# Moving two of the four value tiles behind the next step's keys, unpacking nibbles in four operations, and adding the last rows one block sooner

## The reference

```python
x = x + _layernorm(_L0_attn_ref(_layernorm(x), W_Q, W_K, W_V, W_O, b_Q, b_K, b_V, b_O))
x = x + _layernorm(_L0_ffn_ref(_layernorm(x), gate_W_packed, gate_scales, up_W_packed, up_scales,
                               down_W_packed, down_scales))
# attention: 16 heads of 128, causal softmax
q, k, v = x @ W_Q + b_Q, x @ W_K + b_K, x @ W_V + b_V
z = softmax(where(causal, q @ k.T / sqrt(128), -100000.0)) @ v
out = z @ W_O + b_O
# MLP, 2048 hidden: the weights are 4-bit codes, two to an int word, with a scale per 32
low, high = W_packed & 15, W_packed >> 4 & 15       # low nibble first
W = NVFP4_LUT[interleaved(low, high)] * scales
out = (gelu_tanh(x @ Wg.T) * (x @ Wu.T)) @ Wd.T
```

## Time and profile before

| | |
|---|---|
| median of 3 timed runs | 1555.29 us (1555.06 to 1555.84) |
| the profiled execution: its own time | 1557.55 us |
| the profiled execution: span of the trace | 1555.8 us |
| PE busy | 1539.1 us, 99% of the span |
| DVE busy | 1080.1 us, 69% |
| ACT busy | 985.8 us, 63% |
| POOL busy | 714.2 us, 46% |
| DMA, mean rate | 122 GB/s |
| granted TensorE clock | 0.999 of full speed |

### The profile page before, as it was taken

One profiled execution on the slowest core, in us unless ns is written; L12 is line 12 of the kernel. 1 busy time (PEld: TensorE's weight loads), 2 busy tenths in 40 slices (PEclk: granted clock), 3 DMA queues, 4 the chain that ended last, 5 costly groups with the idle time before them and its releaser, 6 DMA issues.

```text
span 1555.8 us, 25706 instructions
## 1 busy us (share of the span) xinstructions
PE 1539.1 (99%) x8136; PEld 1326.5 (85%) x8136; DVE 1080.1 (69%) x3116; ACT 985.8 (63%) x2449; POOL 714.2 (46%) x1069
## 2 busy tenths in 40 slices
PE   8999999999999999999999999999999999999998
PEld 7888888888888888888888888888788888888887
DVE  5666777777777777677777777757667676675765
ACT  7887777767776777677777776654444444444443
POOL 6673455444455455445445445433333333333333
PEclk9999999999999999999999999999999999999999
DMA  5653444444444444444444444681211121112101
GB/s 161 185 163 101 141 153 136 137 152 146 146 150 139 143 145 154 140 138 147 144 141 142 146 142 148 213 309 63 94 51 60 54 68 39 57 55 68 54 28 41
DMA packets 173415, 190.48 MB, mean 122 GB/s; under 512 B 17888, under 2 KB 143840, under 8 KB 173280
## 3 DMA queue, kind: packets, MB, share of 16 engines
q1 hardware_dynamic: 173280, 188.84, 37.9%
HBM read 105.93 MB, written 82.84 MB: 121 GB/s over the span
## 4 chain that ended last, share of the span: by engine, by line
PE 87%; DMA 4%; ACT 3%; DVE 3%; SPq 2%; issue 1%; POOL 0%; DVEq 0%; ACTq 0%
PE fbank L790 15%; PE fbank L788 15%; PE fbank L789 15%; PE obank L788 7%; PE obank L790 7%; PE obank L789 7%; PE ubank L788 5%; PE ubank L790 5%; PE ubank L789 5%; PE ubank L813 3%; PE fbank L899 3%; DMA turned_scratch<-turned 2%; DMA back<-turned_scratch 1%; SPq L542 1%; ACT probs L674 1%
## 5 line engine op out<-in xcount | busy, mean ns | idle before, releaser
L1378 POOL TENSOR_TENSOR pT_lo<-back,pT_hi 128x512 fp32r<-128x512 f32 x128 | 165.9, 1296 | 284.0 <-ACT pT_hi L742 284.0
L788 PE MATMUL fbank<-xnT_hi,wqk_hi 128*128 128x512 f32 x640 | 249.8, 390 | 0.2 <-DVE xnT_lo L972 0.2
L790 PE MATMUL fbank<-xnT_hi,wqk_lo 128*128 128x512 f32 x640 | 249.4, 390 | 0.0
L789 PE MATMUL fbank<-xnT_lo,wqk_hi 128*128 128x512 f32 x640 | 249.4, 390 | 0.0
L1338 POOL TENSOR_SCALAR probs<-probs,rsum 128x128 f32<-128x128 f32 (+1 forms) x512 | 210.5, 430 | 11.4 <-DVE rsum L995 6.5
L685 ACT ACTIVATE w_raw<-fbank 128x512 f32<-128x512 f32 x128 | 76.6, 598 | 211.9 <-PE fbank L790 211.9
L987 DVE CUSTOM_DVE_ANT_0 probs<-ubank,mask 128x128 f32<-128x128 f32 (+1 forms) x512 | 156.3, 356 | 30.5 <-PE ubank L790 28.2
L1358 POOL TENSOR_TENSOR v_lo<-probs,v_hi 128x512 fp32r<-128x512 f32 x64 | 83.1, 1299 | 175.5 <-ACT v_hi L694 175.5
L655 ACT ACTIVATE zT_hi<-fbank,bias_v 128x512 fp32r<-128x512 f32 x128 | 87.6, 685 | 119.0 <-PE fbank L899 118.9
L1358 POOL TENSOR_TENSOR kT_lo<-probs,kT_hi 128x512 fp32r<-128x512 f32 x64 | 82.7, 1292 | 160.8 <-ACT kT_hi L694 160.8
L1110 DVE SCALAR_TENSOR_TENSOR probs<-w_raw,fbank 128x512 f32<-128x512 f32 x128 | 88.0, 688 | 97.9 <-ACT w_raw L689 94.8
(11 more groups left out here) (168 smaller groups left out, 4513.4 us busy)
## 6 DMA issues: line engine op xcount, KB each, us to landing
turned_scratch<-turned SPq DMA_DIRECT2D x128, 384.0 KB, 2.5
back<-turned_scratch SPq DMA_DIRECT2D x512, 96.0 KB, 2.2
w_raw<-in_w_pairs SPq DMA_DIRECT2D x28, 256.0 KB, 3.1
w_hi_scratch<-w_hi SPq DMA_DIRECT2D x48, 128.0 KB, 2.0
w_lo_scratch<-w SPq DMA_DIRECT2D x48, 128.0 KB, 2.0
x_res<-in_x SPq DMA_DIRECT2D x16, 256.0 KB, 3.0
wqk_hi<-w_hi_scratch SPq DMA_DIRECT2D x16, 256.0 KB, 5.8
wqk_lo<-w_lo_scratch SPq DMA_DIRECT2D x16, 256.0 KB, 5.9
```

Of the source, the lines that this page charges most:

```text
L788: nc.tensor.matmul(out, a[0], b[0], start=start, stop=False, skip_group_check=skip)
L789: nc.tensor.matmul(out, a[0], b[1], start=False, stop=False, skip_group_check=skip)
L790: return nc.tensor.matmul(out, a[1], b[0], start=False, stop=stop, skip_group_check=skip)
L1378: pool.tensor_tensor(lo[:].rearrange("p u b (a j) -> p (u b) a j", j=32), mem.back[m % 2][:, :, 0:2].rearrange("p a u b j -> p (u b) a j") ...
```

## The change

In `step_plan` the last two of the four value tiles leave the end of the value step n (n % 4 == 1) and stand in step n+1 between k and T. This holds from the second group of heads on; the first group (steps 0 and 1) is as it was. The order of PE, ACT and DVE follows from it. `spread` forms both fields with one `(w << 12) | w` in place of a mask-and-shift and a mask-and-or; the other three operations are the same. All 48 pieces are now done at "sum", so that in a value step `spread` stands ahead of v0's `v_lo`. Part 5 of `finish_y` for the first MLP chunk goes from block 16 to block 15, right behind part 4.

```diff
@@ step_plan @@
     plan += [("pT", n - 1), ("scores", n + 1)]
-    return plan + values if n % HG == 1 else plan
+    if n % HG == 2 and n > 2:
+
+        at = plan.index(("T", n))
+        return plan[:at] + values[2:] + plan[at:]
+    return plan + values[:2] if n % HG == 1 else plan
@@ spread @@
         if n:
             dve.wait_ge(s.w4, n)
-        after(dve.tensor_scalar(mem.spread[:], mem.words[:], 0xF0, 12, ALU.bitwise_and,
-                                ALU.logical_shift_left))
-        after(dve.scalar_tensor_tensor(mem.spread[:], mem.words[:], 0xF, mem.spread[:],
-                                       ALU.bitwise_and, ALU.bitwise_or))
+        after(dve.scalar_tensor_tensor(mem.spread[:], mem.words[:], 12, mem.words[:],
+                                       ALU.logical_shift_left, ALU.bitwise_or))
         dve.tensor_scalar(mem.words[:], mem.spread[:], 0x80008, 12, ALU.bitwise_and,
                           ALU.logical_shift_left)
@@ extra @@
         piece = piece_of_step(c * HEADS + j)
-        if piece is not None and place == ("end" if j % HG == 1 else "sum"):
+        if piece is not None and place == "sum":
             spread(piece)
@@ between @@
         if c == 0:
-            finish_at = {10: (-1,), 13: (0, 1), 14: (2,), 15: (3, 4), 16: (5,)}
+            finish_at = {10: (-1,), 13: (0, 1), 14: (2,), 15: (3, 4, 5)}
```

## The result

The changed kernel took 1563.15 us (median of 6 runs, 1561.51 to 1564.79), the kernel before beside it 1555.84 us (6 runs). The ratio is 1.0045 [1.0035, 1.0056]: slower by about 7 us, 5.4 to 8.7. The prediction was 1557.2 us with a range of 1552 to 1564, and slower was the likeliest of the three signs, at 0.45. The time lies in the range, but at its upper end, and outside the forecast's own part of it (1554.5 to 1560): it is in the range because that was drawn to take in most of rival A.

A forecast was written before the change was run, and what follows sets the result against it. PE, busy 1539.1 of 1555.8 us, was taken as the bound, so only its waits count. The terms +8.2 - 4.6 - 0.1 (late restart in step 65) - 1.6 gave +1.9 us: 1557.2 us, range 1552 to 1564.

The forecast's parts named there:

- rival A: Late keys stay because the DMA itself is slow, not because of T's start: +6.6 us, 1561.9 us; chance 0.30.
- `spread` ahead of v_lo: In 28 value steps `spread` delays v0's `v_lo` to +4.13, so PE waits at v0's bank: +8.2 us.
- Loads of the words that might land late: The words `spread` reads might land late in value steps: nothing taken, 2 us for the upper end.
- Late keys: PE's score waits for DVE's `kT_lo`, 5.2 us behind the third step, mostly go as T starts sooner: -4.6 us.
- T's place: T of step n+1 would start 2.4 us before the score matmul instead of 0.57, 1.8 sooner.
- Two value tiles moved, PE's banks: Behind the scores each result still finds the same wait with v2 and v3 a step later: nothing put.
- Last rows: In the MLP the second addition and store come 2.7 us sooner, ending PE's wait for ACT's copy: -1.6 us.
- B: Faster rival: `spread` keeps its quiet pace, 0.94 us, or PE does not wait for `v_lo`; -3.7 us, 1551.6 us; chance 0.15.
- C: Slower rival: POOL's normalising holds `spread`'s first operation for a whole 0.43 us; +11.7 us, 1567.0 us; chance 0.10.

The follow-up runs named there:

- e1: The changed kernel with `spread` in value steps behind v0's `v_lo` instead of ahead of it; 1553.61 us, ratio 0.9982 to the kernel before.
- e2: The kernel before with only the four-operation `spread` and all pieces at "sum", value tiles and last rows unmoved; 1565.49 us, ratio 1.0051.
- e8: The changed kernel with `spread` in its five old operations at the same places; 1574.02 us, ratio 1.0118 to the kernel before.
- e3: The kernel before with only the last rows' second addition (part 5) one block sooner; 1555.93 us, ratio 0.9992.
- e6: The kernel of e1 with five-operation `spread` and the last rows as before, so the moved value tiles alone; 1555.18 us, ratio 0.9997.
- e9: The kernel of e1 with the second pair of standardising operations of the first MLP chunk one block earlier; 1554.05 us, ratio 0.9975 to the kernel before.
- e7: The kernel before with `spread` in four operations at its old places and nothing else; 1555.17 us, ratio 0.9998.
- e5: The kernel of e1 with T of steps n % 4 = 2 held until PE has finished z, except at j = 14; 1560.47 us, ratio 1.0029.
- n1: The kernel before, unchanged, profiled once more; that execution took 1559.3 us.
- n2: The kernel before, unchanged, profiled a further time; that execution took 1557.79 us.

## Why the prediction came out as it did, step by step

**`spread` ahead of v_lo: right, in mechanism and size.** Forecast 8.2 us; measured 7.6 and 8.4 in the two profiles, where the kernel before has 0.1 and twice 0.5, so 7.6 on the mean. v_lo's end was forecast at +4.13 and is at +4.12. Two small errors cancel: PE starts 0.05 us behind v_lo's end and not 0.09, and the restart costs 0.11 and not 0.08. e1 takes the loss away with the place alone, e2 makes it with the place alone, e8 scales it with the block's length.

**Loads of the words that might land late** got nothing in the sum. Right: ahead of the 48 first operations DVE was idle 0.1 us in all.

**Late keys: the term that was mis-sized.** "Of the 5.2 us I take 4.6" was the step that failed. Two things were wrong with it. The 5.2 came from one execution, and such a sum of few waits differs from one execution to the next: the mean of the profiles with the old attention order (three of before, and e3) is 3.4. And the cause named did not go. The new order gives 2.2 and 2.4 in the changed kernel, 0.9, 1.4, 2.3 and 1.5 in e1, e6, e8 and e9, on the mean 1.8. The gain is about 1.6 us, not 4.6, and with a scatter from 2.4 to 5.0 before, this is a rough figure. Nor is it the moved tiles' alone: in the old order with the shorter `spread`, late keys are 1.0 us (e7) and 1.6 (e2), in the new order with the long one 1.4 (e6) and 2.3 (e8). Either part alone goes with about as few as both, so the record can't say whose the gain is.

Why the rest stays can be read at the last two late steps, 124 and 125, which cost 1.0 us before and 1.0 after. PE's first score matmuls of steps 122 to 125 after answer to the last four of the earlier trace rows:

```profile
983.59 0.39 PE L817 MATMUL ubank<-k_early,q_early 128*128 128x128 f32 x2
...
990.00 0.39 PE L817 MATMUL ubank<-k_early,q_early 128*128 128x128 f32 x2
...
996.70 0.49 PE L817 MATMUL ubank<-k_early,q_early 128*128 128x128 f32 x2
...
1003.79 0.49 PE L817 MATMUL ubank<-k_early,q_early 128*128 128x128 f32 x2 [0.42 <-DVE kT_lo L978]
```

The distances are 6.41, 6.70 and 7.09, against 6.41, 6.91 and 6.94 before. T of step 122, the moved one, and the store and return that it sets off:

```profile
981.15 1.03 DVE L1174 STREAM_TRANSPOSE turned<-probs 128x384 f32<-128x384 f32 x2
```

```profile
981.04 0.43 SPq L485 DMA_DIRECT2D wv_lo<-w_lo_scratch  x1
982.20 0.32 SPq L536 DMA_DIRECT2D turned_scratch<-turned  x1
988.22 1.75 SPq L546 DMA_DIRECT2D back<-turned_scratch  x4
990.00 0.44 SPq L528 DMA_DIRECT2D w_hi_scratch<-w_hi  x1
...
991.45 0.63 SPq L522 DMA_DIRECT2D scale<-in_scales  x1
992.18 0.40 SPq L536 DMA_DIRECT2D turned_scratch<-turned  x1
```

T starts 983.59 - 981.15 = 2.44 us ahead of the scores, which is the forecast 2.4. Its store is issued 1.39 us ahead of them. But SP can issue the return only when the store has landed, and that took 6.0 us, where 2.55 is the median of the 31 steps of this kind: six loads of finished MLP weights (into buffers that the last chunk no longer needs), the last at 981.04, went out just ahead of it. The return leaves 988.22 - 983.59 = 4.63 us behind the scores; before, in the same step, it was 4.53 (981.95 against 977.42, by the trace of before). T's lead of 1.9 us is gone, SP's nibble traffic follows the return as before, and the store of step 123 is as late as ever: issued at 992.18, 1.7 us after its transposes ended. That the weights' loads are what the store is behind is read from the order of issue and not tested by itself. For it speaks that in this step all six profiles with the new order and the earlier T have 5.2 to 6.0 us, and the six with the old order and T where it was 2.9 to 4.0; in the first of them the store goes out 2.7 us behind the last load. But loads ahead are not the only cause of a slow store. In steps 34, 90 and 98 SP had issued nothing for 5 us, and it took 4.3 to 4.6 us all the same; step 34 after:

```profile
286.43 0.34 SPq L536 DMA_DIRECT2D turned_scratch<-turned  x1
291.03 1.75 SPq L546 DMA_DIRECT2D back<-turned_scratch  x4
```

Why is open. In the other steps of this kind the return did come 1.9 us sooner in the median (1.01 behind the scores against 2.88), in steps that had not been late.

This also shows a slip in the prediction's reading. The transposes and the late store of the earlier trace rows are those of step 123, which the change does not move; only the return that holds up SP there is of step 122. The distance of 0.57 us is the same in both steps, so the forecast of T's place came out right all the same.

At step 125 something else stands ahead too: DVE does a layer norm's standardising (L1037, 0.83 us for two) between the inversion and `qT_lo`, which the change leaves there.

```profile
1001.33 0.17 DVE L999 RECIPROCAL rsum<-sums 128x2 f32<-128x2 f32 x1 [0.71 <-ACT probs L678]
1001.41 0.83 DVE L1037 TENSOR_SCALAR stream<-w_raw,mv,rstd 128x256 f32<-128x256 f32 x2
1002.28 0.48 DVE L978 SCALAR_TENSOR_TENSOR qT_lo<-fbank,bias_q,qT_hi 128x256 fp32r<-128x256 f32 x1
1002.98 0.75 DVE L978 SCALAR_TENSOR_TENSOR kT_lo<-fbank,bias_k,kT_hi 128x512 fp32r<-128x512 f32 x1 [0.22 <-ACT k_early L670]
```

Steps 5 and 13, late in both profiles of the changed kernel, are not of this kind: DVE has no such part there, and its `qT_lo` waits 0.56 us for ACT's `q_early`. Why that is late stays open.

**Two value tiles moved, PE's banks: right.** No wait for v2's `v_lo` or for `v_late` has come, in any kernel.

**Last rows: right in kind, 1.1 us and not 1.6.** The 0.5 missing is the collision of the second addition with POOL, which e9 removes. The prediction added 0.69 us to DVE's block; it was 1.8. It also had only the store in front of ACT's copy; with the store early enough, ACT's own activations stand there.

**The sum.** With the terms as measured, +7.6 - 1.6 - 1.1 = +4.9 us; the ratio says 7.0, and 5.4 at least. So 2.1 us, or 0.5 at least, are not accounted for by these three. The profiles don't show it: the two of the changed kernel are 5.2 us over the three of the kernel before, on the mean of their own times, which is near 4.9. What the timed runs have beyond that stays open; the fall of the clock in the start-up comes and goes in both kernels, and no profile tells how often in the timed runs. Of the 5.1 us between 1.9 forecast and 7.0 measured, 3.0 are the late keys and 0.5 the last rows; `spread` itself was put 0.6 too high.

**The rivals.** A (+6.6, 1561.9) came nearest to the time. Its claim that the late keys have nothing to do with T is refuted by e5, where a later T makes more of them, but its picture, in which landings of DMAs decide, fits steps 122 to 124 and the scatter of n1 and n2 better than the forecast's. B fell: v_lo did not end at +3.90. C fell too: the first operation took 0.37 us beside POOL and was not held for a whole operation of POOL's.

## What to carry to other kernels

Work may be put ahead of an operation only within its slack, read on the clock of the engine that waits for it: here v0's `v_lo` had 4.08 - 3.37 = 0.71 us, and a block of 1.17 us behind an inversion that leaves it 0.4 idle cost 0.2 us in most of 28 steps, more where the inversion came late, and 0.27 on the mean. Waits shorter than the listed length of a matmul are read from the distances between starts, since the view of waits showed 1.0 of 7.6 us. A gain that rests on a handful of waits in one profile wants two or three profiles before it gets a number, and a transfer that is started sooner wants a look at what was issued just ahead of it.

## What the runs showed of the hardware that was not expected

- A VectorE addition of two SBUF tiles (128x512, 0.69 us alone) took 1.78 us when it started 0.24 us after POOL's subtraction had, and 0.69 when it started 0.23 us before; then POOL's took 1.62 instead of 1.30. The Trainium skill, "SBUF — State Buffer", section "Who interferes with whom", says that a VectorE instruction with two SBUF inputs contends with a GpSimd one that reads SBUF, and that the one that comes second is blocked. At this place the trace agrees, within 0.15 us of a full hold.
- Beside POOL's normalising the cost is small: `spread`'s first operation 0.37 us against 0.28 in e1's quieter place (medians of the value steps), its last 0.37 against 0.29, and from the start of the block to that of `v_lo` 1.17. In the same block of five operations (e8) that stretch is 1.51 us in step 41.
- `v_lo`, with one input in PSUM, takes 0.66 to 0.69 us everywhere, with an operation of POOL beside it or not.
- A matmul that a semaphore releases barely late costs more than its lateness: the next one follows after 0.34 us instead of 0.23. Over 28 steps that made 3.1 of the 7.6 us.
- From the issue of the store of one head's transposed probabilities to the issue of its return it is 2.4 us in most steps, 6.0 behind six weight loads, and 4.3 to 4.6 in some steps (34, 90, 98) with nothing issued in the 5 us ahead.
- TensorE's granted clock fell in the start-up of 9 of 14 profiles, of both kernels (0.50 from 35 to 37 us in n1, where 512-column matmuls came every 0.43 us and not every 0.23), after a wait of PE of 1.8 to 2.6 us, and stayed at 1.00 in the others after waits of 1.6 to 2.5 us.
